# Transformer layer on eight cores: paired statistics matmuls behind one wait, and the attention store in two pieces

## The reference

```python
x = x + _layernorm(attn(_layernorm(x)))        # 16 heads of 64, softmax(q k^T * 0.125) v, then Wo
x = x + _layernorm(ffn(_layernorm(x)))
# ffn(x), every _tlin(x, w, s) = (x @ w.T) * s
h = jax.nn.silu(_tlin(x, w1_w, w1_s)) * _tlin(x, w2_w, w2_s)          # 1024 -> 4096
h = jax.nn.gelu(_tlin(h, h1_w, h1_s), approximate=False)              # 4096 -> 4096
h = jax.nn.gelu(_tlin(h, h2_w, h2_s), approximate=False)              # 4096 -> 4096
return _tlin(h, w3_w, w3_s)                                           # 4096 -> 1024
# _layernorm(x) = (x - mean) / sqrt(var + 1e-5) over the features
```

## Time and profile before

| what | value |
|---|---|
| two runs | 8662.44 and 9508.28 us, median 9085.36 us |
| profiled execution | 8488.09 us |
| its span, slowest core | 8486.5 us |
| spans of the cores | 8450.1 to 8486.5 us |
| TensorE busy | 7642.1 us, 90% of the span |
| ScalarE busy | 3057.9 us, 36% |
| VectorE busy | 1263.4 us, 15% |
| GpSimd busy | 629.9 us, 7% |

### The profile page before, as it was taken

The page is one execution under the profiler, slowest core; times in us unless marked ns, Lnnn a source line. Parts: engine busy times, 40 slices in busy tenths (PEclk is TensorE's granted clock), DMA queues, the critical chain, the costliest instruction groups (busy, mean ns, idle before and its releaser), DMA issues.

```text
span 8486.5 us, 98456 instructions; the slowest of 8 cores (8450.1 to 8486.5 us)
## 1 busy us (share of the span) xinstructions
PE 7642.1 (90%) x34757; PEld 3097.9 (37%) x35264; DVE 1263.4 (15%) x1971; ACT 3057.9 (36%) x3341; POOL 629.9 (7%) x908
## 2 busy tenths in 40 slices
PE   4688888888888877999999999999999999999998
PEld 1323232222322223444444444444444444444443
DVE  4312021120211003012002002002002102102101
ACT  2287877878778881011111111111111111111110
POOL 3100000000000000010001001001001001001000
PEclk6789899888988888999999999999999999999999
DMA  2154235545451004445435435435444544544533
GB/s 44 16 101 87 54 71 101 103 86 114 96 106 24 4 5 135 145 154 159 153 138 161 162 138 160 164 137 158 167 139 153 167 144 148 168 145 141 170 140 128
DMA packets 629806, 1015.25 MB, mean 120 GB/s; under 512 B 424544, under 2 KB 432736, under 8 KB 562784
## 3 DMA queue, kind: packets, MB, share of 16 engines
q1 hardware_dynamic: 510944, 539.12, 20.7%
q0 software_dynamic: 118400, 469.81, 20.7%
HBM read 998.32 MB, written 119.54 MB: 132 GB/s over the span
## 4 chain that ended last, share of the span: by engine, by line
PE 73%; ACT 13%; issue 5%; DVE 4%; DMA 3%; POOL 1%; ACTq 0%; DVEq 0%; another core or an unknown queue 0%; SPq 0%; POOLq 0%
PE psum L854 21%; PE psum L878 19%; ACT pT L533 10%; PE psum L909 5%; PE psum L816 5%; PE psum L825 5%; PE psum L544 4%; PE psum L525 4%; PE psum L548 3%; PE psum L301 3%; DMA h2sl<-h2B 2%; PE psum L327 1%; PE psum L693 1%; ACT recT L561 1%; ACT rbc L557 1%
## 5 line engine op out<-in xcount | busy, mean ns | idle before, releaser
L533 ACT ACTIVATE pT<-psum,negM 128x1024 bf16<-128x1024 f32 x2048 | 2124.2, 1171 | 537.1 <-PE psum L525 527.6
L878 PE MATMUL psum<-g,h2sl 128*128 128x512 bf16 x8029 | 1799.3, 381 | 35.7 <-DMA h2sl<-h2B 18.9
L854 PE MATMUL psum<-h,h1sl 128*128 128x512 bf16 x8029 | 1761.4, 379 | 18.1 <-DVE h L834 9.0
L878 PEld LDWEIGHTS psum<-g,h2sl 128*128 128x128 bf16 x8192 | 802.1, 98 | 1003.4 <-issue 56.9
L854 PEld LDWEIGHTS psum<-h,h1sl 128*128 128x128 bf16 x8192 | 800.6, 98 | 978.9 <-issue 15.8
L525 PE MATMUL psum<-qP,kP 64*128 64x512 bf16 x4096 | 852.3, 414 | 137.3 <-DVE rbc L581 65.8
L544 PE MATMUL psum<-pT,vP 128*65 128x512 bf16 x2048 | 886.3, 433 | 56.8 <-DVE att_st L591 20.5
L548 PE MATMUL psum<-pT,vP 128*65 128x512 bf16 x2048 | 841.5, 411 | 0.0
L883 ACT ACTIVATE h<-psum,h2s_sb 128x512 bf16<-128x512 f32 x256 | 175.9, 687 | 1662.9 <-PE psum L878 1645.4
L859 ACT ACTIVATE g<-psum,h1s_sb 128x512 bf16<-128x512 f32 x256 | 175.9, 687 | 1533.5 <-PE psum L854 1533.4
L525 PEld LDWEIGHTS psum<-qP,kP 64*128 64x128 bf16 x4096 | 226.9, 94 | 1019.5 <-issue 1013.1
(11 more groups left out here) (119 smaller groups left out, 3563.3 us busy)
## 6 DMA issues: line engine op xcount, KB each, us to landing
h2sl<-h2B POOLq DMA_DIRECT2D x256, 1024.0 KB, 5.6
h1sl<-h1B SPq DMA_DIRECT2D x256, 1024.0 KB, 4.9
w1sl<-w1B SPq DMA_DIRECT2D x256, 256.0 KB, 3.0
w2sl<-w2B SPq DMA_DIRECT2D x256, 256.0 KB, 3.0
w3sl<-w3B POOLq DMA_DIRECT2D x128, 512.0 KB, 5.0
h1sl<-h1T POOLq DMA_DIRECT2D x32, 512.0 KB, 9.4
h2sl<-h1T POOLq DMA_DIRECT2D x32, 512.0 KB, 14.3
h1B<-h1sl SPq DMA_DIRECT2D x32, 512.0 KB, 10.1
```

Of the source, the lines that this page charges most:

```text
L533: kb.plan("s", lambda s, ping=ping, st=st, nm0=nm0: s.activation(out=pT[:, ping * 1024: ping * 1024 + 1024], in_=psum[:, 2 * st * 512: (2 ...
L854: m = t.matmul(PB(bk), h1sl[jp][:, i * 128:(i + 1) * 128], hB[i][:], start=(i == 0), stop=(i == HC - 1))
L878: m = t.matmul(PB(bk), h2sl[jp][:, i * 128:(i + 1) * 128], g1B[i][:], start=(i == 0), stop=(i == HC - 1))
```

## The change

The store of att_st is issued as two DMAs of 64 x 512 elements, one for each head, instead of one of 64 x 2 x 512. At the three places with paired sum matmuls, the two steps become one: both matmuls stand behind the waits of both, only the second increments the semaphore, and both banks count as written by that step.

```diff
@@ plan_fin_tt @@
                 kb.dma("g", f"Dg_ast{stp}", lambda g, p=p, q0=q0, stp=stp: g.dma_start(
-                    out=attnS[p * 128:(p + 1) * 128, q0:q0 + QG]
-                    .rearrange("(h r) t -> r h t", h=2),
-                    in_=att_st[stp][0:64, :].rearrange("r (h t) -> r h t", t=QG)),
+                    out=attnS[p * 128:p * 128 + 64, q0:q0 + QG],
+                    in_=att_st[stp][0:64, 0:QG]),
+                    reads=[f"ast{stp}"])
+                kb.dma("g", f"Dg_ast{stp}", lambda g, p=p, q0=q0, stp=stp: g.dma_start(
+                    out=attnS[p * 128 + 64:(p + 1) * 128, q0:q0 + QG],
+                    in_=att_st[stp][0:64, QG:2 * QG]),
                     reads=[f"ast{stp}"])
@@ head_thunks, t_st @@
-                    kb.plan("t", lambda t, j=j: t.matmul(
-                        PB(4), ones_b[:, :], projb[j][:],
-                        start=(j == 0), stop=(j == DC - 1), skip_group_check=True),
-                        reads=[f"projb{j}", "ones_b"], writes=["pb4"])
-                    kb.plan("t", lambda t, j=j, xp=xp: t.matmul(
-                        PB(5), ones_b[:, :], sqT[:, xp * 512:(xp + 1) * 512],
-                        start=(j == 0), stop=(j == DC - 1), skip_group_check=True),
-                        reads=[f"sqT{xp}", "ones_b"], writes=["pb5"])
+                    kb.plan("t", [
+                        lambda t, j=j: t.matmul(
+                            PB(4), ones_b[:, :], projb[j][:],
+                            start=(j == 0), stop=(j == DC - 1), skip_group_check=True),
+                        lambda t, j=j, xp=xp: t.matmul(
+                            PB(5), ones_b[:, :], sqT[:, xp * 512:(xp + 1) * 512],
+                            start=(j == 0), stop=(j == DC - 1), skip_group_check=True)],
+                        reads=[f"projb{j}", f"sqT{xp}", "ones_b"],
+                        writes=["pb4", "pb5"])
@@ the tail of a group @@
             for j in range(DC):
-                kb.plan("t", lambda t, j=j: t.matmul(
-                    PB(2), ones_b[:, :], projb[j][:], start=(j == 0), stop=(j == DC - 1)),
-                    reads=[f"projb{j}", "ones_b"], writes=["pb2"])
-                kb.plan("t", lambda t, j=j: t.matmul(
-                    PB(3), ones_b[:, :], hB[j][:], start=(j == 0), stop=(j == DC - 1)),
-                    reads=[f"h{j}", "ones_b"], writes=["pb3"])
+                kb.plan("t", [
+                    lambda t, j=j: t.matmul(
+                        PB(2), ones_b[:, :], projb[j][:],
+                        start=(j == 0), stop=(j == DC - 1)),
+                    lambda t, j=j: t.matmul(
+                        PB(3), ones_b[:, :], hB[j][:],
+                        start=(j == 0), stop=(j == DC - 1))],
+                    reads=[f"projb{j}", f"h{j}", "ones_b"], writes=["pb2", "pb3"])
```

More of the change, by code:

```diff
@@ L755, in t_x2b @@
                     xp = j % 2
[L756 to L763, removed]
+                    kb.plan("t", [
+                        lambda t, j=j, xp=xp: t.matmul(
+                            PB(4), ones_b[:, :], x2b[xp][:],
+                            start=(j == 0), stop=(j == DC - 1), skip_group_check=True),
+                        lambda t, j=j, xp=xp: t.matmul(
+                            PB(5), ones_b[:, :], sqT[:, xp * 512:(xp + 1) * 512],
+                            start=(j == 0), stop=(j == DC - 1), skip_group_check=True)],
+                        reads=[f"x2b{xp}", f"sqT{xp}", "ones_b"],
+                        writes=["pb4", "pb5"])
                 th.append(t_x2a)
```

## The result

| | before | after |
|---|---|---|
| all runs, median (lowest to highest) | 8768.7 us (8478.9 to 9636.1), 40 runs | 8695.0 us (8511.1 to 9668.8), 41 runs |
| ratio to before | | 1.0037, 95% interval 1.0024 to 1.0051 |
| profiled execution | 8488.1 us | 8527.4 us |
| span, slowest core | 8486.5 us | 8525.9 us |
| spans, mean of the eight cores | 8466.5 us | 8511.4 us |

The change costs 0.37%, some 31 us: well outside its interval, well inside the 2%. In part of the executions of every kernel here the cores of one die, or of both, run at a lower clock and take some 100 to 1150 us longer; the ratios leave those out, and the medians of all runs say nothing about the change. The profiled executions lie 39 us apart, the means of their cores 45 us.

What follows compares the result with a forecast made beforehand. TensorE, busy 7642 of 8486.5 us, was taken as the bound. Terms 6.0 + 3.0 + 14.0 + 2.0 + 2.4 + 0.6 = 28 us on the profiled 8488.1 gave 8516 us, range 8440 to 9085.

Steps and rivals of the forecast that it cites:

- likeliest case: The sum of the terms, 8516 us, with its own range 8480 to 8560 us; chance 0.66.
- Chunks 4 to 7: First statistics in h2: one matmul of 0.216 us moves behind the square's wait at 28 stalls, 6.0 us.
- Chunk 0: Second statistics: the moved matmul takes up to 0.43 us at the lowered clock, 7 times, 3.0 us.
- Tails and end: Group tails: pair step 0.74 us, mean 2.0 us late; 14.0 us over seven tails, 2.0 us at the program's end.
- Head of group 0: Two statistics with nothing beside them, the mean waiting for the whole pair: 1.2 us each, 2.4 us.
- the store: Last att_st store before the barrier: its second half leaves one issue later, 0.6 us.
- squares-cover-it rival: Pair's own wait is cheaper or slack absorbs the mean's delay; only moved matmuls count, 14 us, 8502 us; chance 0.15.
- 0.15 us between an end and a start: Tail pairs: wait from one matmul's end to the next's start, the least certain number; if it vanished, sum 18 us.
- clock rival: Two: clock set back at 36 gaps, 50 us more, 8566 us, 0.07; 1.2 GHz through 28 rounds, 8709 us, 0.02.
- case of nothing or faster: Pairs' own waits prove free and h2's waits for loads shrink in a few groups; four gone give 8480 us; chance 0.10.
- late loads of h2: h2 loads TensorE waits for, 2.06 us in one place, could arrive in time and give back some of the sum.

Runs made afterwards that it cites:

- three traces with head pairs: The changed kernel, the same once more, and the kernel before with only the heads' pairs joined; groups 5107.7, 5112.0 and 5108.3 us.
- four without: Kernel before, and it with only the store split, only the tail pairs joined, or these without waits among them; groups 5096.3 us on the mean.
- the experiment without the wait: Kernel before with only the tail pairs joined and no pair waiting for the end of the pair ahead; profiled 8501.0 us.
- three re-orderings and VectorE: Kernel before with first squares a round earlier, second sums a round later, tail sums moved into w3 rounds, odd chunks' residual arithmetic on VectorE; ratio 0.9906.
- odd chunks on VectorE: Kernel before with the residual arithmetic of the odd chunks on VectorE instead of GpSimd; profiled 8462.1 us, ratio 0.9964.
- three re-orderings: Kernel before with first squares one round earlier, second sums one round later, tail sums moved into the w3 rounds; profiled 8432.4 us, ratio 0.9934.

## Why the prediction was right or wrong

Against the profiled execution the forecast was 28 us more, 8516; measured were 31 us by the ratio and 39 us between the profiled executions. The likeliest case's own range, 8480 to 8560, holds the profiled 8527.4. Term by term:

- **Chunks 4 to 7, 6.0 us.** 6.0 to 6.1 us in rounds 17 to 20 in each of the three traces with these pairs behind stalls and GpSimd's arithmetic as before. Where there is no stall, nothing.
- **Chunk 0, 3.0 us.** 2.8 to 4.1 us in round 22. The lowered clock is what makes it more than one matmul: 1.4 us where the clock stays up.
- **Tails and end, 14.0 + 2.0 us.** 14.9 + 2.2 us. The step of a pair, 0.74 us, was right to the hundredth. Mis-sized was the start: the first pair begins 1.11 us after the eviction, not 1.00, with one wait list for both matmuls, and that is most of the 0.13 us a tail in 2.15 against 2.0. The step that the whole chain through mean and silu is late, and that TensorE stands for it, held.
- **Head of group 0, 2.4 us, and the store, 0.6 us.** Together 2.9 to 3.1 us between the last product of the attention stage and the first silu. The store was put too high: from its issue to the first load behind the barrier it is 0.2 us more, on the mean of the cores. From the first mean of this head to the second it is 1.0 to 1.3 us more, as forecast for one of the two statistics; the other can't be told from the scatter.
- **What the sum did not have.** The groups are 13 us longer on the mean of three traces with head pairs than of four without, not 9. The mean waits for weights are 18.4 us with them and 15.9 without, 2 us and more of the rest, though one kernel without head pairs has 18.8. I had named those waits only as a gain; where the rest exactly comes from stays open.

The squares-cover-it rival fell: it took the squares' pace for the pairs', and the experiment without the wait gave it back only when the wait was gone. One bound was worked out wrongly beside it: without the 0.15 us between an end and a start, a pair's step would still be 0.216 + 0.38 = 0.60 us, longer than the squares' 0.52, and the sum 20 us instead of 18. Neither clock rival came: mean granted clock of the cores 0.944 to 0.945 after, 0.944 to 0.947 before, and the round behind each of the 28 stalls at full speed. The case of nothing or faster fell with the ratio's interval.

Two steps failed. One is the step from the sum to the statement. I wrote that the range should reach from 8440 to 9085 because the two runs shown lay at 8662 and 9508, and so gave a figure that says nothing about a change of this size: 8516 us beside the median of 9085 reads as a gain of 6%, and measured was a loss of 0.37%. What bears on the change is the profiled execution's 8488.1 us and the ratio. I also leaned on 2% as what can be told from no change. The measurement resolves 0.14%, the sum was 0.33%, and the forecast should have said "slower, by 0.3%", since every term of it had the same sign. The other is in the sum, and small: the late loads of h2 "could arrive in time behind a slower TensorE and give back some of it". Nothing was given back; the groups, put at 9 us, cost 13. That 28 and 31 us agree so well is in part luck, since the scatter of the stages is as large as what the sum left out.

## What to carry to other kernels

Joining two accumulation steps into one saved nothing here where their waits were already met, and where they were not it cost three times: the first matmul moved behind the later operand, the next step waited for the end of both, and every reader of the first bank waited for the second. Before joining steps, look in the timeline for what lies between them; before removing a stall, look which queue's issue it hides. A stall in which an engine waits for a producer recorded in the same round is better cured by recording the producer one round earlier, which here gave back 42 us in the h2 rounds for an edit of a few lines.

## What the hardware showed that I had not expected

- VectorE's float32 operations of 512 columns took 1.5 us beside GpSimd's arithmetic and 0.69 us without it. Moving GpSimd's share onto VectorE as well, more work for the same engine, made the chain at chunk 0 shorter and the kernel 0.36% faster.
- A matmul of 512 columns that waits for the end of another starts 0.14 to 0.15 us after the recorded end in the tails. In the head of group 0 of the changed kernel it is 0.15 us before one pair and 0.23 us before the next, in turn; why is not shown.
- The length of a pause alone did not say whether the clock falls. A wait for h2sl of 2.06 us (before, 3828.46) and one of 2.37 us (three re-orderings and VectorE, 3816.08) were followed by a round of 7.07 us at a granted clock of 1.00. One of 2.15 us (odd chunks on VectorE, 3814.08) and one of 2.28 us (three re-orderings, 3821.97) were followed by 8.75 us, at 0.69 and 0.53 in its first 3 us. The forecast had read from the 2.06 us alone that such a pause leaves the clock as it is.
- The attention stage of unchanged code differs by up to 7 us from execution to execution on the mean of eight cores, and by 27 to 34 us between the cores of one execution. Of a change worth 30 us, the stages that it touches tell more than the time.
